# Mixture-of-experts block and attention conv on one core: the scatter's pause split in two, and the attention weights kept in PSUM

## The reference, cut to what matters

```python
# layer 0
x = depthwise_conv7x7(x) + bias; x = layernorm_over_channels(x)
logits = xf @ Wg + bg; topv, topi = top_k(logits, 2); wts = softmax(topv)
# tokens in order of priority fill the slots of their experts, cap = 15680 each
buf = zeros(E * cap + 1, C).at[slot].set(xrep)              # the scatter
h = gelu(eb @ W1 + b1); y = h @ W2 + b2                      # 8 experts
contrib = yf[slot] * gate                                    # the gather
x = input + x + layer_scale * moe
# layer 1
x_h, x_w = pooled means over columns and rows
y = h_swish(bn(w1 @ concat(x_h, x_w) + b1))
a_h = sigmoid(wh @ y[:, :h] + bh); a_w = sigmoid(ww @ y[:, h:] + bw)
out = conv3x3(x * a_w * a_h, wc); out = bn(out); out = silu(out)
```

## Time and profile before

| | |
|---|---|
| median of 3 runs | 6246.16 us (6243.88 to 6246.7) |
| profiled execution, its own time | 6245.02 us |
| its span in the profile | 6243.3 us |
| granted TensorE clock, mean | 0.89 |
| busy PE, DVE, ACT, POOL | 79%, 39%, 24%, 59% of the span |

### The profile page before, as it was taken

The page is one execution under the profiler, slowest core; times in us unless marked ns, Lnnn a source line. Parts: engine busy times, 40 slices in busy tenths (PEclk is TensorE's granted clock), DMA queues, the critical chain, the costliest instruction groups (busy, mean ns, idle before and its releaser), DMA issues. The chain is left out here.

```text
span 6243.3 us, 66489 instructions
## 1 busy us (share of the span) xinstructions
PE 4951.5 (79%) x20662; PEld 2758.2 (44%) x20662; DVE 2408.8 (39%) x4673; ACT 1506.8 (24%) x3672; POOL 3685.7 (59%) x3630
## 2 busy tenths in 40 slices
PE   8999999111898797898779878378878788888788
PEld 3566559110454444454444444134444444444444
DVE  0012227993222222222222222455555555555553
ACT  2233337330332232333223323011111111111111
POOL 0000000005787787788778775777777777777773
PEclk9999999555999898999889989689989899999889
DMA  8877769842333333332323322333333222222210
GB/s 169 185 184 195 194 168 284 277 159 79 101 110 103 101 107 94 90 92 87 87 82 95 89 83 59 118 94 99 103 113 93 83 79 81 81 81 85 95 49 32
DMA packets 840400, 711.27 MB, mean 114 GB/s; under 512 B 596073, under 2 KB 681711, under 8 KB 836091
## 3 DMA queue, kind: packets, MB, share of 16 engines
q1 hardware_dynamic: 666362, 466.30, 27.4%
q0 software_dynamic: 109312, 139.69, 8.1%
q10 hardware_dynamic: 64512, 102.79, 4.9%
HBM read 440.11 MB, written 385.75 MB: 132 GB/s over the span
## 5 line engine op out<-in xcount | busy, mean ns | idle before, releaser
L1077 POOL DMA_INDIRECT y_ring<-ye,index_o x1568 | 1733.2, 1105 | 462.3 <-issue 460.4
L754 POOL DMA_INDIRECT xe<-chunk,index x1568 | 1539.6, 982 | 477.3 <-issue 477.3
L1110 PE MATMUL cp<-padded,taps_o 128*128 128x448 f32 x4032 | 1663.6, 571 | 63.7 <-DVE padded L1298 63.7
L1110 PEld LDWEIGHTS cp<-padded,taps_o 128*128 128x128 f32 x4032 | 801.1, 203 | 832.3 <-issue 797.7
L882 ACT ACTIVATE hid<-hid_ps,b_cols 128x448 f32<-128x448 f32 x1120 | 709.3, 633 | 1632.8 <-PE hid_ps L836 1534.6
L844 PE MATMUL y_ps<-hid,w_sb 128*128 128x448 f32 x2240 | 956.5, 573 | 0.4 <-DVE yt L907 0.4
L836 PE MATMUL hid_ps<-xt,w_sb 128*128 128x448 f32 x2240 | 891.5, 541 | 1.5 <-DVE xt L901 1.5
L474 POOL MEMSET zeros<- 98x512 f32 x1 | 0.5, 525 | 1109.2 <-POOLq L105 1109.2
L1253 DVE SCALAR_TENSOR_TENSOR z<-y_ring,gates,z 128x128 f32<-128x128 f32 x1568 | 434.5, 346 | 555.5 <-DMA y_ring<-ye,index_o 538.9
L1176 ACT ACTIVATE outb<-cp,shift,s 128x448 f32<-128x448 f32 x224 | 162.1, 724 | 1912.2 <-PE cp L1110 1912.2
L901 DVE COPY xt<-xt_ps 128x448 f32<-128x448 f32 x280 | 174.9, 625 | 1148.5 <-PE xt_ps L827 1145.9
(11 more groups left out here) (192 smaller groups left out, 3736.7 us busy)
## 6 DMA issues: line engine op xcount, KB each, us to landing
xe<-zeros SPq DMA_DIRECT2D x16, 3920.0 KB
rows_in<-xe SPq DMA_DIRECT2D x280, 224.0 KB, 2.6
ye<-rows_out SPq DMA_DIRECT2D x280, 224.0 KB, 2.3
xin<-in_x_dram SPq DMA_DIRECT2D x256, 196.0 KB
conv<-rows ACTq DMA_DIRECT2D x256, 196.0 KB
pix<-conv SPq DMA_DIRECT2D x224, 224.0 KB, 5.0
xn<-hat SPq DMA_DIRECT2D x112, 448.0 KB, 4.3
chunk<-xn POOLq DMA_DIRECT2D x112, 448.0 KB, 3.8
```

Source lines behind the costliest of these rows:

```text
L754: pool.indirect_dma_start(out=xe[:, :], out_offset=bass.IndirectOffsetOnAxis(ap=index[ch][:, c, j:j + 1], axis=0), in_=chunk[ch][:, j * C: ...
L1077: pool.indirect_dma_start(out=y[ch][c][:, j * C:(j + 1) * C], out_offset=None, in_=ye[:, :], in_offset=bass.IndirectOffsetOnAxis(ap=index[ ...
L1110: last = pe.matmul(cp[i % 2][:, 0:HB * W], taps[:, t, :], padded[b][:, img, hb * HB + kh:hb * HB + kh + HB, kw:kw + W], start=(t == 0), st ...
```

## The change

Two edits that have nothing to do with each other.

- Scatter: `LULL` goes from 3000 to 1500 columns, and `rest` is called twice a chunk: once after the 8th of the 14 indirect transfers (after `j` = 3) and once where it stood. Each `rest` first waits until the fill before it is done.
- Output: `weigh` is no tile of SBUF any more but columns 384 to 495 of the PSUM bank `cpre`. The instructions that write it (ACT) and read it (DVE) are the same.

```diff
-LULL = 3000
+LULL = 1500
...
                                 in_=chunk[ch][:, j * C:(j + 1) * C], in_offset=None,
                                 bounds_check=limit, oob_is_err=False).then_inc(scattered[ch], 16)
+                        if j == CHK // 2:
+                            rest(2 * n)
                     if n:
 
                         pool.wait_ge(scattered[(ch - 1) % NCHK], (g + (1 if ch else 0)) * PER_PAIR)
                         pool.sem_inc(chunks_scattered, 1)
-                    rest(n)
+                    rest(2 * n + 1)
...
-        weigh = sb("weigh", [C, A])
...
         cpre = ctx.enter_context(nc.psum_tensor("cpre", [128, 512], F32))
+        weigh = cpre[:, 384:384 + A]
```

## The result

The changed kernel took 6096.9 us, median of 4 runs (6095.73 to 6099.29). The kernel before, run beside it, took 6245.02 us (6243.33 to 6246.7). The ratio is 0.9763 [0.9746, 0.9780]: 148 us faster, where 152 were forecast (6094). The profiled execution took 6095.88 us, with a span of 6094.1 us and a mean clock of 0.899.

The account below looks back on a forecast made before the run. POOL, issuing indirect transfers, was taken to bound the kernel. From 6245.0 us, products -146.1, tail -3 and fills -2.8 gave 6093.1, or 6094 us as median, range 6070 to 6118 for 8 in 10; chance 0.87.

Parts of the forecast that it names:

- What bounds the kernel: Scatter and gather stretches: POOL waits for nobody, so every microsecond on it counts until PE or DVE lacks slack.
- The products, -146.1 us: Output stage: products with `weigh` in PSUM stop holding POOL, removing the whole excess of 62 gathers, -146.1 us.
- remnant of 12.8 us: Gathers: part of the 158.9 us excess outside the 62 held ones, put down to small ones of other kinds.
- The cost of a product with a PSUM input, 0: Output products on DVE: reading one input from PSUM costs nothing extra; other end 6.4 us each, +6 us once.
- What is late next: Gather stretch: nobody takes POOL's place; at least 11 us of `tp_done` distance stay, 146 come off PE's 400.9 us wait.
- The tail, -3 us: End of the run: PE idles 3 us and stays warm, so last turn and 36 matmuls save -3 us (-5 to 0).
- The fills, -2.8 us: Scatter stage: shorter end fills give -141.7 us, the new middle fills cost +138.9 us, sum -2.8 us.
- No scatter is held, so the pause in the middle has no stall to cure.: Scatter stage: scatters take 1052 ns at most, so the middle fill cures no stall.
- still held: Rival, output gathers: the product's remaining SBUF input and output still hold POOL; 6242 us, chance 0.05.
- held for longer: Rival, output gathers: slower PSUM reads, 2.0 ns a column, still hold POOL; 6430 us, chance 0.03.
- partly bound elsewhere: Rival, gather stretch: PE or DVE takes the bound, half of the 146 us comes back; 6167 us, chance 0.05.

Follow-up runs that it names:

- e1: Kernel before with only `weigh` moved to PSUM, one fill of 3000 columns per chunk kept: 6642.51 us, ratio 0.9853 to the kernel before.
- e12: Changed kernel plus a pause of six 220-column memsets per output chunk, second product's weights a_h back in SBUF: 6420.09 us, ratio 1.0282 to the kernel before.
- e6: Changed kernel plus one extra DVE `tensor_scalar` (summed x 2.0, one SBUF input) before each image's products: 6550.26 us, ratio 0.9561 to the kernel before.
- e4: Changed kernel plus one extra DVE product per image with both inputs in SBUF (summed x summed): 6555.73 us, ratio 0.9712 to the kernel before.
- e2: Changed kernel with `weigh` back in SBUF, so only the two fills of 1500 columns remain: 6658.1 us, ratio 0.9847 to the kernel before.
- e7: Changed kernel without any fill in the scatter: 7996.7 us, ratio 1.165 to the kernel before.
- e9: The changed kernel again, unaltered, in another batch: 6546.95 us, ratio 0.9573 to the kernel before.
- e10: Changed kernel with only the second product's weights a_h in SBUF, a_w in PSUM, run in e9's batch: 6649.69 us, ratio 0.9733 to the kernel before.
- e3: Changed kernel with only the second product's weights a_h in SBUF, a_w in PSUM, run in e4's batch: 6658.23 us, ratio 0.9861 to the kernel before.
- e5: Changed kernel plus one extra DVE product per image with one input in PSUM (summed x a_w): 6604.36 us, ratio 0.9643 to the kernel before.
- e11: Changed kernel plus a pause of five 280-column memsets behind every 14 output gathers: 6335.69 us, ratio 0.9259 to the kernel before.

## Why the prediction was right

- *What bounds the kernel.* Right: POOL's chain before and after, and its busy time in the gathers fell by 142.0 us where the stretch fell by 142.1. Nothing was given back.
- *The products, -146.1 us.* The mechanism is shown: e1 alone frees POOL, and in e12 one product holds it and the other does not. The prediction's sentence "an instruction with one SBUF input does not hold POOL" is too wide, though: e6's `tensor_scalar` has one and does hold it. All 62 holds are gone, worth 146.1. The stretch gave 142.1, since new, smaller ones appeared. Beside the 14 back-to-back instructions of `z` (L1255), whose inputs `y_ring` and `z` are both in SBUF, 8 gathers take 1.7 to 2.4 us, against 4 before. Of the forecast's remnant of 12.8 us "of other kinds", 3.5 us were those four; the rest was less than 0.3 us at any one gather. Timeline of DVE and POOL:

```profile
5193.75 3.98 DVE L1255 SCALAR_TENSOR_TENSOR z<-y_ring,gates,z 128x128 f32<-128x128 f32 x14
5194.83 1.71 POOL L1079 DMA_INDIRECT y_ring<-ye,index_o  x1 [0.31 <-issue]
```

- *The cost of a product with a PSUM input, 0.* Right, and the nearest row was the earlier trace rows:

```profile
L1298 DVE TENSOR_TENSOR padded<-summed,cpre x32: 3411/3422/3424, 4021.5 to 6036.3; 128x3136 f32<-128x3136 f32 x32
```

  3422 ns against 3427 ns with both inputs in SBUF (e4's and e12's rows). So the 2.0 ns a column of the earlier trace rows do not come with a PSUM input as such; whether L1266's stride or its form makes them was not tried.
- *What is late next.* Nothing, as forecast. The smallest distance from the turn of chunk n-3 to POOL's first gather of chunk n fell from 21.6 to 16.1 us; at least 11 were said to be left. PE's waiting for `z` fell from 400.9 us to 314.7, not to about 250. All 146 us had been taken off this wait, but PE's busy time fell as well, from 1738.70 to 1689.93 us at a clock of 0.90 after 0.88, and 142.1 - 48.8 = 93 us are all that its waits could give.

```profile
PE tp L1132 <- DVE z L1255: 314.7, 44, 18.5
```

- *The tail, -3 us.* 2.9, by the mechanism named: PE waits 0.63 us for the last `z`, turns it in 0.98 and runs the 36 matmuls in 13.70, against 7.41, 1.75 and 15.86. The granted clock was 1.00 from 6011 to 6027 us, where it had been 0.84 from 6158 to 6176. The idle time had been put at 3 us.

```profile
6011.56 0.98 PE L1132 MATMUL tp<-ident_o,z 128*128 128x128 f32 x7 [0.63 <-DVE z L1255]
6012.39 13.70 PE L1112 MATMUL cp<-padded,taps_o 128*128 128x448 f32 x36
```

- *The fills, -2.8 us.* 2.6, which is closer than the terms were: errors of both signs cancelled. A fill takes 1.379 us on average and not 1.350, since the forecast took the slope between `lull` and the memset of another tile (1792 columns); between `lull`'s own 1500 and 3000 columns it is 0.83 ns a column. The end of a chunk gives 1.254 us in place of 1.277, that is 139.2 us in 111 chunks and not 141.7. In the middle, from one scatter to the next, 2.510 us pass where 1.284 did, so it costs 1.226 and not 1.24, 137.3 us and not 138.9: the scatter behind the fill takes 0.98 us and not 1.01, and the fill begins 0.017 us before the record of the scatter in front of it ends, which together outweighs the longer fill and its gap. -139.2 + 137.3 = -1.9 us; the other 0.7 us are a few ns less at the other scatters.
- *"No scatter is held, so the pause in the middle has no stall to cure."* True of the trace that was read, and wrong as a general sentence. It looked for the stall on POOL, while in the long batches the fills act on the other engines. Where signals come late, the split is worth 67 us (e1 against e2), and without any fill the kernel ran 17% longer than the kernel before (e7). In the result's batch both kernels have none to cure.
- The rivals: *still held* and *held for longer* fall with the 150 unheld gathers, *partly bound elsewhere* with the 142.1 of 142.0 us.

**What stays open.** Why signals, and PE's own instructions, are late in three batches and timely in two; e1 to e4 and e12 carry the same chip number, so that number does not explain it. The only thing shown is that a pause of POOL removes most of it. In the long batches the change is worth about what its parts are: with e1 0.9853 and e2 0.9847 the product is 0.970, and e4, both edits and an extra product that holds POOL for 26 us, has 0.971. e9's 0.957 is from another batch. No trace of the kernel before was taken in a long batch, so this is not split into stages. Of the differences there, 90 us between e1's and e2's gather stretches and 55 us between e9 and e10 are not holds of POOL and have no cause. Whether the fills are needed at all where signals are timely was not tried.

## What to carry to other kernels

When POOL issues indirect transfers without a break and is the bound, look at the longest of them, not the mean, and see what DVE runs at their end; of an instruction with both inputs in SBUF put one in PSUM, which costs DVE nothing here and returned the whole hold; an instruction with a single SBUF input may hold POOL too (e6). Before removing a pause on such an engine, count how late the other engines start after what they wait for, since a pause that looks idle may be what lets them through. And compare a kernel only with one that ran in the same batch: the same code took 6245 and 6849 us.

## What the runs showed of the hardware

- A `tensor_tensor` with both inputs in SBUF holds an indirect transfer that begins beside it, and not one that had already begun. Gathers that began up to 0.009 us after a product's start (0.023 in e4) took 1.00 to 1.02 us, and all from 0.147 us on were held (0.097 in e12). Every held one ends 0.87 to 0.89 us after the product (e4, e12), which is the rest of its 1.00 us.
- A `tensor_scalar` with one SBUF input, at 0.57 ns a column, holds POOL too (5 of 5 in e6, and a sixth that had begun before it). I had not reckoned with it; the Trainium skill, "SBUF — State Buffer", section "Who interferes with whom", does name `tensor_scalar` among the instructions that can take the shared ports, and the runs agree. It also held the two gathers of e6 that had begun 0.01 and 0.70 us before it, until 0.12 us after its end, which no product did.
- POOL's own copy of 14 slot numbers a partition, 0.2 us with all operands in SBUF, is held by the same instructions: all 94 that began inside a product with two SBUF inputs (26 in e2, 26 in e3, 15 in e4, 27 in e10) and all 9 inside the `tensor_scalar` of e6, each until 0.06 to 0.07 us after its end; none of the 23 inside e9's products with PSUM.
- Products with one PSUM input never held a gather: 150 gathers in the changed kernel, 32 at the extra product of e5, 163 in e11.
- The same section of the Trainium skill infers that a `tensor_tensor` does not stall the making of descriptors. The runs decide against it: all 62 gathers that began 0.1 us or more after the start of a product were held in the kernel before, and 31 of 31 at one product of e12.
- ACT writes the same 56 columns to PSUM in 282 ns (307 to SBUF).
- While POOL issues indirect transfers without a break, DVE or ACT can start up to 39 us after PE's result is there in the output and up to 34 us in the experts (e7), in some batches, and a PE matmul that waits for nothing up to 2.6 us after the one before (e2). In others, with the same code, none of these delays is over 0.2 us. A pause of 1.9 us per 14 transfers brought the longest down to 4.0 us in the output (e11).
- In the experts, in one batch, one pause of 2.6 us per 14 transfers left 101 of 280 late (e1) and two of 1.4 us left 3 to 13 (e2, e3, e4), so their spacing counts there and not only their sum. In the two other long batches two of 1.4 us left 65 to 74 late, none by more than 5.6 us.
